# Attention and mixture-of-experts kernel: early shared loads, gated halves, an overflow branch moved ahead of the late stage, late sums in 2 KB pieces

## The chip, the cores and the metric

The kernel runs on one core of one Trainium2 chip, as one launch. The metric is device time in microseconds of that core. A measurement of this kernel can tell a change of about 0.3% from no change.

## What is computed

The input is x of shape (4, 1024, 256) in float32. Cut to what matters, the reference is:

```python
# power attention, 8 key heads, 2 query heads each, d = 128
a = where(causal, (q @ k.T * scale)**2 * exp(gate), 0)
y = (a @ v) / (sum(a) + 1e-6)
x = layernorm(x + y @ Wc + bc)
# mixture of experts over N = 4096 rows: 64 experts, top 6, capacity 768, F = 176
scores = softmax(x @ gate_w.T);  w, idx = top_k(scores, 6);  w = w / (sum(w) + 1e-20)
y = sum over the chosen experts of w * (silu(x @ wg.T) * (x @ wu.T)) @ wd.T
# shared expert over all rows, FS = 352
s = (silu(x @ sg.T) * (x @ su.T)) @ sd.T
out = layernorm(x + y + s)
```

## The kernel before, in words

Every product of float32 numbers is split into a rounded high part and the rest. `product` (L936) makes three TensorE passes for one product, and `down_passes` (L945) five for the down projection, where two rest parts share the array. All tiles sit in eight banks of PSUM: banks 0 to 5 hold gate and up results, three for each of two hidden units, and banks 6 and 7 are the spare pair, used in turn by everything else.

`schedule()` writes one list, `order`, of tasks, by hand. Each engine has a program (`sp_program`, `pe_program`, `act_program`, `dve_program`, `pool_program`) that walks the same list and runs those tasks that it has a part in. So the order of the list is the order on every engine, and what an engine waits for stands in its own instructions, as semaphore waits through `Once`. A task that waits holds up all that follows on its engine.

The stages in order are these.

- **Attention.** Units of scores and values, for four batches of eight heads. In the last two heads the routing of the batch before, and of the first half of the last batch, runs in the background, one step for each unit: statistics, normed rows, their transpose `x1t` (stored to DRAM as `x1t_dram`), logits, softmax, top 6, one-hot counts, slots, and for each half the steps `again` and `send`, whose rows POOL scatters into the experts' `slots` (L2284).
- **Shared stage.** Six blocks m of 512 rows. Each block has two hidden units k = 2m and 2m + 1, 12 in all. `up(k)` is three parts of six passes (TensorE). `hidden(k, part)` is the gate, in four parts: part 0 silu of the first 128 hidden rows (ACT), part 1 multiplication (DVE) and high part (ACT), part 2 silu of the last 48 rows (ACT), multiplication and rest of the first part (DVE), part 3 high and rest of the last 48 (`hb`, ACT then DVE). `shared_end(m)` is two `shared_down` of 20 matmuls each, eviction by ACT into `y_e`, and the store. `shared_in(m)` loads a block's transposed rows; XE = 4 buffers hold blocks 0 to 3, of which block 0 is loaded in the last attention units and blocks 1 to 3 after `attention_over` (L1138). Between these, `route_to(...)` runs the routing of the second half of the last batch, and two steps rank the experts by their counts.
- **Expert stage.** 68 places; at each, `up`, `hidden`, the transposes of the next expert's rows, and the `down` of the one before. ACT weighs and evicts the results, and POOL adds them to the output's rows by indirect DMA (L2294). At place 8 `rank_counts` finds whether any expert has more rows than its place holds, into `over_count`, and POOL loads that number into a register (L2303).
- **Late stage.** Two more blocks of the shared expert (ML = 2, units KL to KR - 1), in the order up, hidden, up, hidden, two `late_down`.
- **Overflow.** `overflow` (L2479 to L2497) on PE, ACT, DVE and POOL: wait for `o_done`, load the count (POOL has it already), branch. With a count over 0 the rest rows are worked; else `skip` sets the semaphores. For these inputs the count is 0, so the way taken is the far one, over the whole body.
- **Block sums.** SP loads each block's two partial results (L1188 to L1190), POOL adds them (L2365), DVE makes statistics (L2201 to L2226), ACT norms (L1758 to L1767), SP stores. There are six blocks of four rows per partition and four of two; the last four take rows in an order that makes the pieces 1 KB.

Of the kernel before, what the change touches and what calls it, by code (L numbers as in the profile page):

```python
# [182 lines left out]
def schedule():  # L183
# [81 lines left out]
    early_at = {12: ("raw_in", SHARED[0]), 13: ("raw_in", SHARED[1]), 14: ("shared_in", 0), 17: ("split_hi", SHARED[0]),  # L265
# [49 lines left out]
    for u, (n_, g, s) in enumerate(UNITS_ALL):  # L315
# [94 lines left out]
    assert not background  # L410

    second = route_steps(B)
    tail = [item[1:] for item in late]
    assert tail == [("project", HEADS - 1, NG - 2), ("turn", HEADS - 1, NG - 1), ("project", HEADS - 1, NG - 1)], tail
# [27 lines left out]

    catch_up()
    up(0, 0)
    do("experts_begin")
    send_all()
    hidden(0, 0)
# [4 lines left out]
    hidden(0, 1)  # L452
    on_spare("project", HEADS - 1, NG - 2)
    hidden(0, 2)
# [3 lines left out]
    hidden(0, 3)  # L458
    route_to("stat0")
    up(1, 1)  # L460
    do("add", HEADS - 1, NG - 1)
    for m in range(1, XE):
        do("shared_in", m)
    route_to("std")
    up(1, 2)
    hidden(1, 0)
    route_to("store")
    up(2, 0)
    route_to("x1t0")
    hidden(1, 1)  # L470
    up(2, 1)
    route_to("logit0")
    hidden(1, 2)
    route_to("x1t1")
    up(2, 2)
    hidden(1, 3)
    route_to("logit1")
    do("rank_keys")
    shared_end(0)
    on_spare("rank_experts")  # L480
    do("raw_in", MAINS[0])
    route_to("softmax0")
    up(3, 0)
    hidden(2, 0, 1)
    route_to("softmax1")
    up(3, 1)
    route_to("max")
    up(3, 2)
    hidden(2, 2, 3)
    route_to("index")  # L490
    up(4, 0)
    route_to("chosen0")
    up(4, 1)
    hidden(3, 0, 1)
    up(4, 2)
    route_to("chosen1")
    hidden(3, 2, 3)
    shared_end(1)
    do("raw_in", MAINS[1])
    route_to("weight1")  # L500
    hidden(4, 0, 1)
    up(5, 0)
    route_to("count")
    hidden(4, 2, 3)
    up(5, 1)
    route_to("slots")
    route_to("send0")
    up(5, 2)
    hidden(5)
    route_to("send1")  # L510
    assert not second
    for m in range(2, M1):
        if m + 1 < M1:
            for k in (2 * m + 2, 2 * m + 3):
                up(k)
                hidden(k)
        shared_end(m)
        if m in (2, 3):
            do("split_hi", MAINS[m - 2])
            for part in range(3):  # L520
                do("split_lo", MAINS[m - 2], part)
# [20 lines left out]
    for place, x_id in enumerate(SEQ):  # L542
# [4 lines left out]
        if place == 8:  # L547
            on_spare("rank_counts")
            do("load_count")
# [27 lines left out]
    if not ML:  # L577
        down(SEQ[-1], (0, 1))
    for d in range(ML):
        for k in (KL + 2 * d, KL + 2 * d + 1):  # L580
            up(k)
            hidden(k)
            if k == KL:
                down(SEQ[-1], (0, 1))
# [48 lines left out]
def build(nc, xT, x, wall, wvall, wg, gw, bc, wffn, table, out):  # L633
# [45 lines left out]
    N_SPARE = len(spare)  # L679

# [17 lines left out]
    with ExitStack() as ctx:  # L698
# [52 lines left out]
        over_count = sb(ctx, "over_count", [1, 1], I32)  # L751
# [220 lines left out]

        def rows_of(x_id):
# [53 lines left out]
        def sp_program(e):  # L1027
# [81 lines left out]
            def route(p, name):  # L1109
# [4 lines left out]
                elif name[:3] == "x1t":  # L1114
# [3 lines left out]
                    e.dma_start(x1t_dram[0, :, :, ts], f32(x1t_hi[:, :, :])).then_inc(s_x1t_out, 16)  # L1118
                    once.wait_ge(*out_of(("route", p, name)))
                    e.dma_start(x1t_dram[1, :, :, ts], f32(x1t_lo[:, :, :])).then_inc(s_x1t_out, 16)  # L1120
# [62 lines left out]
            def rows_of_block(whole, n):  # L1183
                at = sum(BLOCK_ROWS[:n]) * P
                order_ = "(p j) c -> p j c" if n < M1 else "(j p) c -> p j c"
                return whole[at:at + BLOCK_ROWS[n] * P, :].rearrange(order_, p=P)
# [26 lines left out]
        def pe_program(e):  # L1213
            once = Once(e)

# [1345 lines left out]
```

## Time and profile before

| what | value |
|---|---|
| time, median of 3 runs | 2263.62 us (2263.26 to 2268.72) |
| the profiled execution's own time | 2266.61 us |
| its span in the trace | 2264.8 us |
| TensorE busy in the span | 2151.7 us, 95% |
| mean granted clock of TensorE | 0.975 of full |
| VectorE, ScalarE, GpSimd busy | 1286.2, 1157.8, 751.3 us |
| shared stage, as it is cut below | 1619.0 to 1742.5 us |
| expert stage, from the first down to the last add | 1760 to 2214 us |

Busy time of an engine is the sum of its instructions; a line of the 40 slices of the page shows where in the span it is low. TensorE is at nine tenths or more in nearly every slice; it falls to seven or eight in the slices of the shared stage, and to two in the last one, where only the block sums are left. An engine name with a q behind it (POOLq, ACTq) is its sequencer: branches, register loads and semaphores.

### The profile page before, as it was taken

What the parts mean: (1) busy time and instruction counts of PE and PEld (TensorE: products, weight loads), DVE (VectorE), ACT (ScalarE), POOL (GpSimd) and SP (SyncE); (2) the same over time, 40 slices, a digit from 0 to 9 for tenths busy, and PEclk for the clock granted to TensorE, in tenths of its full rate; (3) what the DMA queues carried; (4) which work ended last, traced back from release to release, by engine and by line L of the source; (5) the groups of instructions that cost most, each with busy time, mean ns of one, the idle gap of its engine ahead of it and who ended that gap; (6) DMA issues with size and microseconds to landing.
All of it is one profiled execution on the core that took longest, in us unless ns stands there. A gap on an engine that the chain in (4) does not pass through costs nothing.

```text
span 2264.8 us, 38662 instructions
## 1 busy us (share of the span) xinstructions
PE 2151.7 (95%) x14567; PEld 1967.5 (87%) x14570; DVE 1286.2 (57%) x2851; ACT 1157.8 (51%) x2201; POOL 751.3 (33%) x751
## 2 busy tenths in 40 slices
PE   8999999999999999999999999999879899999992
PEld 6999998999989899888989898998767889999982
DVE  4444444454666445465644556545654688888865
ACT  4544545444444445444444444444324677877764
POOL 3121112100004510000452002430214578878883
PEclk9999999999999999999999999999889999999996
DMA  5876722122112411211241211322244789999966
GB/s 171 335 274 263 294 102 71 46 63 71 43 52 98 138 49 54 81 35 59 92 141 53 80 53 54 104 78 70 76 165 150 194 214 235 235 229 235 230 126 230
DMA packets 148180, 302.30 MB, mean 133 GB/s; under 512 B 20336, under 2 KB 85616, under 8 KB 147984
## 3 DMA queue, kind: packets, MB, share of 16 engines
q1 hardware_dynamic: 106496, 247.34, 32.3%
q0 software_dynamic: 41056, 51.96, 11.5%
q8 instruction: 117, 1.92, 0.3%
q14 instruction: 79, 0.65, 0.1%
q10 hardware_dynamic: 432, 0.44, 0.1%
HBM read 160.57 MB, written 142.67 MB: 134 GB/s over the span
## 4 chain that ended last, share of the span: by engine, by line
PE 84%; DVE 7%; ACT 4%; issue 3%; DMA 1%; POOL 1%; SPq 0%; ACTq 0%; DVEq 0%; POOLq 0%
PE bank L936 51%; PE bank L1331 21%; PE bank L945 7%; PE bank L1344 2%; PE bank L1448 2%; DVE ub L1876 1%; DVE bank L2061 1%; DVE bank L2058 1%; ACT silu_b L1664 0%; POOL slots L2284 0%; DVE stats L2210 0%; ACT wf_hi L1648 0%; ACT q_hi L1591 0%; ACT xe_hi L1675 0%; ACT x1t_hi L1633 0%
## 5 line engine op out<-in xcount | busy, mean ns | idle before, releaser
L1331 PEld LDWEIGHTS bank<-v,a 128*128 128x128 f32 x4608 | 605.2, 191 | 43.6 <-ACT a L1615 0.5
L1331 PE MATMUL bank<-v,a 128*128 128x129 f32 x4608 | 618.4, 275 | 0.3 <-ACT a L1615 0.3
L2294 POOL DMA_INDIRECT y_part<-y_e,row_token x234 | 360.2, 1539 | 123.9 <-issue 62.6
L2267 POOL TENSOR_TENSOR decay_all<-decay_all,tab 128x128 f32<-128x128 f32 x128 | 59.5, 465 | 918.6 <-DMA decay_all<-decay_dram 918.3
L1611 ACT ACTIVATE a<-bank,c_s 128x512 f32<-128x512 f32 x384 | 263.1, 686 | 183.6 <-PE bank L936 170.8
L1615 ACT ACTIVATE a<-ub 128x512 f32<-128x512 f32 (+1 forms) x256 | 133.8, 523 | 376.9 <-DVE ub L1876 370.6
L2284 POOL DMA_INDIRECT slots<-rows,slot_u x192 | 188.5, 982 | 336.9 <-DVE slot_u L2041 154.2
L936 PE MATMUL bank<-q_hi,k_hi 128*128 128x512 f32 (+1 forms) x640 | 262.6, 410 | 7.5 <-DVE ub L1876 7.5
L1855 DVE TENSOR_TENSOR q_lo<-bank,q_hi 128x512 fp32r<-128x512 f32 x128 | 88.5, 692 | 271.4 <-ACT q_hi L1591 271.3
L936 PE MATMUL bank<-q_lo,k_hi 128*128 128x512 f32 (+1 forms) x640 | 238.3, 372 | 0.0
L936 PE MATMUL bank<-q_hi,k_lo 128*128 128x512 f32 (+1 forms) x640 | 237.2, 371 | 0.0
L936 PE MATMUL bank<-xe_hi,wf_hi 128*128 128x512 f32 (+8 forms) x504 | 192.3, 382 | 18.5 <-DVE hb L2066 9.2
L936 PE MATMUL bank<-xe_lo,wf_hi 128*128 128x512 f32 (+8 forms) x504 | 185.6, 368 | 0.0
L936 PE MATMUL bank<-xe_hi,wf_lo 128*128 128x512 f32 (+8 forms) x504 | 185.4, 368 | 0.0
L936 PE MATMUL bank<-xt_hi,w_hi 128*128 128x512 f32 x384 | 166.4, 433 | 2.4 <-DVE acc L1916 1.3
L936 PE MATMUL bank<-wc_hi,yt_hi 128*128 128x256 f32 x512 | 155.1, 303 | 3.6 <-DVE yt_lo L1906 3.6
L1916 DVE TENSOR_TENSOR acc<-bank,acc 128x512 f32<-128x512 f32 x128 | 88.2, 689 | 116.9 <-PE bank L936 116.7
L936 PE MATMUL bank<-xt_hi,w_lo 128*128 128x512 f32 x384 | 151.2, 394 | 0.0
L936 PE MATMUL bank<-xt_lo,w_hi 128*128 128x512 f32 x384 | 150.8, 393 | 0.0
L1876 DVE TENSOR_TENSOR ub<-bank,em 128x512 f32<-128x512 f32 (+1 forms) x256 | 140.8, 550 | 16.4 <-PE bank L936 8.8
L936 PE MATMUL bank<-wc_hi,yt_lo 128*128 128x256 f32 x512 | 145.3, 284 | 0.0
L936 PE MATMUL bank<-wc_lo,yt_hi 128*128 128x256 f32 x512 | 145.1, 283 | 0.0
(231 smaller groups left out, 4766.3 us busy)
## 6 DMA issues: line engine op xcount, KB each, us to landing
slots<-acc SPq DMA_DIRECT2D x64, 816.0 KB, 7.8
w_raw_f<-in_wffn SPq DMA_DIRECT2D x68, 624.0 KB, 5.1
decay_all<-decay_dram SPq DMA_DIRECT2D x128, 128.0 KB, 3.1
xr<-slots SPq DMA_DIRECT2D x18, 544.0 KB, 5.5
xr<-slots SPq DMA_DIRECT2D x20, 476.0 KB, 5.3
w_hi<-w_dram SPq DMA_DIRECT2D x24, 384.0 KB, 4.4
w_lo<-w_dram SPq DMA_DIRECT2D x24, 384.0 KB, 5.1
wc_hi<-wc_dram SPq DMA_DIRECT2D x24, 256.0 KB, 2.6
```

What stands on the lines that cost most here:

```text
L936: ins = e.matmul(dst, a, b, start=first and i == 0, stop=last and i == len(passes) - 1, skip_group_check=True)
L945: ins = e.matmul(dst, a, b, start=first and n_ == 0 and p_ == 0, stop=n_ == len(steps) - 1 and p_ == len(passes) - 1, skip_group_check=True)
L1331: ins = e.matmul(dst[:, tt, r, :], a32[u % NA][:, r, t0:t0 + P], v[n % 3][:, s, :], start=(s == 0 and r == 0), stop=(s == 2 * g + tt), ski ...
L1344: ins = e.transpose(ps[:, r, tt * P:(tt + 1) * P], yn[j % YR][:, tt, r, :], ident)
L1611: e.activation(squares, score_bank(u)[:, 0:R * w].rearrange("p (r t) -> p r t", r=R), ACT.Square, scale=c_s[b % 2][:, g * (g - 1) + s, h:h ...
L1615: e.activation(squares, ub[masked_nth[u] % 2][:, :, 0:w], ACT.Square).then_inc(s_sq)
L1855: e.tensor_tensor(lo, bank[6 + m % 2][:, :], f32(hi), ALU.subtract).then_inc(s_out_of[m % 2])
L1876: e.tensor_tensor(ub[mine % 2][:, :, 0:w], score_bank(u)[:, 0:R * w].rearrange("p (r t) -> p r t", r=R), decay.unsqueeze(1).to_broadcast([ ...
L1916: e.tensor_tensor(part, bank[6 + m % 2][:, :].rearrange("p (t c) -> p t c", c=C), part, ALU.add).then_inc(s_out_of[m % 2])
L2267: e.tensor_tensor(arg[:, GROUP:GROUP + P], arg[:, P:GROUP], mask, ALU.add)
L2284: e.indirect_dma_start(out=slots, out_offset=bass.IndirectOffsetOnAxis(ap=slot_u[:, j, k:k + 1], axis=0), in_=rows[:, j, :], in_offset=Non ...
L2294: e.indirect_dma_start(out=y_part[part], out_offset=bass.IndirectOffsetOnAxis(ap=token, axis=0), in_=y_rows, in_offset=None, bounds_check= ...
```

## The change

The first shared rows are loaded earlier. `shared_in(1)` goes to attention unit 37 and waits only for the last scores, `shared_in(2)` goes right ahead of the first `up`, and `shared_in(3)` behind the last `add`. The last part of the first half's routing (`again1`, `send1`) is held back from the attention units and done behind `shared_end(0)`. In the shared stage `gated` takes the place of `hidden`: both silus in part 0, both multiplications in part 1 on DVE, high parts on ACT and rests on DVE behind. The two transposes `x1t0` and `x1t1` of the second half stand side by side, the second in the buffers `yt_hi[0]` and `yt_lo[0]`, and the order of `up`, `gated`, `shared_end` and the routing steps is written anew; both ranking steps stand behind the last `send`. From block 2 on the eviction of a shared down also waits for all stores of `x1t`.

`over_count` becomes `no_rest`, 1 where the count is 0. All four engines load it at place 8 of the expert stage. PE, ACT and DVE branch ahead of the late stage, and POOL behind its last add: the way with `no_rest` stands directly behind the branch, holds the late stage and the block sums, and ends in a jump over the other way, which holds the same again with the overflow between. The late stage's order becomes up, hidden, last expert down, up, hidden, up, two `late_down`, hidden, up, hidden, two `late_down`. The late hidden units are written by tile, so that a partition holds neighbouring rows and the late pieces of sums and output are 2 KB.

```diff
--- before.py
+++ after.py
-    early_at = {12: ("raw_in", SHARED[0]), 13: ("raw_in", SHARED[1]), 14: ("shared_in", 0), 17: ("split_hi", SHARED[0]),
+    early_at = {12: ("raw_in", SHARED[0]), 13: ("raw_in", SHARED[1]), 14: ("shared_in", 0), 37: ("shared_in", 1), 17: ("split_hi", SHARED[0]),
...
-        elif background and u >= step_from:
+        elif background and u >= step_from and background[0] != (B - 1, "again1"):
...
+    def gated(k, *parts):
+        for part in parts or range(4):
+            do("gated", k, part)
+
     catch_up()
+    do("shared_in", 2)
     up(0, 0)
     do("experts_begin")
     send_all()
     up(0, 1)
     on_spare("turn", HEADS - 1, NG - 1)
     do("turn_lo", HEADS - 1, NG - 1)
     up(0, 2)
+    gated(0, 0)
     on_spare("project", HEADS - 1, NG - 2)
+    gated(0, 1)
     up(1, 0)
     do("add", HEADS - 1, NG - 2)
     on_spare("project", HEADS - 1, NG - 1)
     route_to("stat0")
+    gated(0, 2, 3)
     up(1, 1)
     do("add", HEADS - 1, NG - 1)
+    do("shared_in", 3)
     route_to("std")
     up(1, 2)
+    gated(1, 0)
     route_to("store")
+    gated(1, 1)
     up(2, 0)
     route_to("x1t0")
+    on_spare("route", *second[1])
+    x1t1 = second.pop(1)
+    gated(1, 2, 3)
     up(2, 1)
     route_to("logit0")
     up(2, 2)
     route_to("logit1")
+    route_to("softmax0")
+    shared_end(0)
+    for step in background:
+        route_step(*step)
+        send_all()
+    gated(2, 0)
+    route_to("max")
+    gated(2, 1, 2, 3)
+    up(3)
+    route_to("index")
+    route_to("chosen0")
+    gated(3, 0)
+    up(4)
+    gated(3, 1, 2, 3)
+    route_to("chosen1")
+    shared_end(1)
+    route_to("weight1")
+    gated(4, 0)
+    up(5, 0)
+    gated(4, 1, 2, 3)
+    route_to("count")
+    up(5, 1, 2)
+    route_to("slots")
+    route_to("send0")
+    up(6)
+    gated(5)
+    shared_end(2)
+    route_to("send1")
+    assert not second
     do("rank_keys")
     on_spare("rank_experts")
     do("raw_in", MAINS[0])
     do("raw_in", MAINS[1])
+    up(7)
+    gated(6)
+    for m in range(3, M1):
+        up(2 * m + 2) if m + 1 < M1 else None
+        gated(2 * m + 1)
+        shared_end(m)
         if m + 1 < M1:
+            up(2 * m + 3)
+            gated(2 * m + 2)
+        if m in (3, 4):
+            do("split_hi", MAINS[m - 3])
             for part in range(3):
+                do("split_lo", MAINS[m - 3], part)
...
+    do("late",)
+    for k in range(KL, KR):
+        up(k)
+        if k == KL:
             hidden(k)
-            if k == KL:
-                down(SEQ[-1], (0, 1))
-        if d + 1 < ML:
-            do("late_in", d + 1)
-        for pair in range(MAIN // GROUP):
-            on_spare("late_down", d, pair)
+            down(SEQ[-1], (0, 1))
+            continue
+        if (k - KL) % 2 == 0:
+            for pair in range(MAIN // GROUP):
+                on_spare("late_down", (k - KL) // 2 - 1, pair)
+        hidden(k)
+        if (k - KL) % 2 and (k - KL) // 2 + 1 < ML:
+            do("late_in", (k - KL) // 2 + 1)
+    for pair in range(MAIN // GROUP):
+        on_spare("late_down", ML - 1, pair)
     return order, spare
...
+        def rows_first(k):
+            return MT if k >= KL and k < KR else 1
+
+        def in_order(by):
+            return (lambda a: a.rearrange("p (t j) -> p t j", j=by)) if by > 1 else (lambda a: a)
+
+        def by_tile(by):
+            return (lambda a: a.rearrange("p (j t) -> p t j", j=by)) if by > 1 else (lambda a: a)
...
-                if m:
+                if m >= XE:
                     attention_over(once)
+                elif m:
+                    once.wait_ge(s_scores, len(UNITS_ALL))
+                    if m > 1:
+                        values_over(once)
...
+                m, half = (n, None) if n < M1 else (M1 + (n - M1) // 2, (n - M1) % 2)
+                in_rows = whole[m * MAIN:(m + 1) * MAIN, :].rearrange("(p j) c -> p j c", p=P)
+                return in_rows if half is None else in_rows[:, 2 * half:2 * half + 2, :]
...
+            def load_count():
+                nonlocal fits
+                once.wait_ge(c_count, 1)
+                fits = e.value_load(no_rest[0:1, 0:1], min_val=0, max_val=1)
...
+            passed = dict(once.passed)
+            with e.If(fits > 0):
+                late()
+            with e.Else():
+                once.passed = passed
+                late()
+                overflow(e, once, over_body, over_skip, over_settled)
...
+            def gated(k, part):
+                b0, i = 3 * (k % 2), k % HS
+                if part == 0:
+                    if k == 0:
+                        values_over(once)
+                    once.wait_ge(c_gu, 3 * k + 1)
+                    if k:
+                        once.wait_ge(c_h, 2 * k)
+                    e.activation(silu_a[:, :], bank[b0][:, :], ACT.Silu).then_inc(c_silu)
+                    once.wait_ge(c_gu, 3 * k + 3)
+                    e.activation(silu_b[:, :], bank[b0 + 2][0:FB, :], ACT.Silu).then_inc(c_silu)
+                elif part == 1:
+                    once.wait_ge(c_h, 2 * k + 1)
+                    hidden_free(once, k)
+                    e.activation(ha_hi[i][:, :], bank[b0 + 1][:, :], ACT.Copy).then_inc(c_hh)
+                elif part == 2:
+                    once.wait_ge(c_h, 2 * k + 2)
+                    once.wait_ge(c_zero, HS)
+                    e.activation(hb[i][0:FB, :], bank[b0 + 2][0:FB, :], ACT.Copy).then_inc(c_hh)
...
+                if m_ >= 2:
+                    once.wait_ge(s_x1t_out, 16 * 2 * NG * B)
...
-                e.tensor_copy(over_count[:, :], rank_col[0:1, 0:1]).then_inc(c_count)
+                e.tensor_scalar(no_rest[:, :], rank_col[0:1, 0:1], 0.0, None, ALU.is_equal).then_inc(c_count)
...
+            with e.If(fits > 0):
+                e.sem_inc(o_done, E)
+                sums()
...
+        def x1t_of(p, k):
+            return (yt_hi[0], yt_lo[0]) if (p, k) == (B, 1) else (x1t_hi, x1t_lo)
...
```

## Rows read from the trace of the kernel before

**Rows 1.** The page, part 4: shares by engine of the chain that ended last

```profile
PE 84%; DVE 7%; ACT 4%; issue 3%; DMA 1%; POOL 1%; SPq 0%; ACTq 0%; DVEq 0%; POOLq 0%
```

**Rows 2.** Windows: us, length, busy PE PEld DVE ACT POOL, PEclk, DMA share, GB/s

```profile
1619.00:1742.50 123.50, 100.00 (x530) 84.94 (x527) 68.19 (x141) 44.00 (x72) 49.38 (x53) 0.88 0.42 146
```

**Rows 3.** Waits of PE, shared stage: waiting line, releaser, us, times, longest

```profile
PE bank L936 <- DVE hb L2066: 9.2, 3, 4.6
PE bank L936 <- DMA xe_lo<-x1t_dram: 7.7, 1, 7.7
PE bank L936 <- DVE x1t_lo L1955: 3.5, 1, 3.5
```

**Rows 4.** Chain of work, shared stage: start, us, what, matmuls

```profile
1640.37 2.93 PE bank L936 x6
...
1680.51 6.57 PE bank L945 x40
...
1706.71 4.80 PE bank L945 x40
...
1724.61 8.30 PE bank L936 x36
```

**Rows 5.** Timeline, one hidden unit, first silu to last rest

```profile
1717.88 0.58 ACT L1657 ACTIVATE silu_a<-bank 128x512 f32<-128x512 f32 x1
...
1721.99 0.68 DVE L2066 TENSOR_TENSOR hb<-bank,hb 48x512 fp32r<-48x512 f32 x1
```

**Rows 6.** Timeline, first units of the shared stage

```profile
1629.04 1.95 POOL L2291 MEMSET hb<- 112x512 f32 x4
...
1635.67 1.38 DVE L1948 TENSOR_SCALAR rows<-acc,mv,rstd 128x256 f32<-128x256 f32 x4
```

**Rows 7.** Chain, two of DVE's routing steps

```profile
1672.78 0.97 DVE onehot L1991
...
1676.76 1.53 DVE chosen L1999
```

**Rows 8.** Chain, first expert weights behind the shared stage

```profile
1749.25 3.88 DMA w_raw_f<-in_wffn
```

**Rows 9.** Timeline of POOL, last of the second half's 24 scatters

```profile
1727.06 1.29 POOL L2284 DMA_INDIRECT slots<-rows,slot_u  x1 [0.30 <-issue]
```

**Rows 10.** Timeline, line L2303 and chain: the count's way at place 8

```profile
1800.46 0.27 PE L1481 MATMUL bank<-rank_hot,count_col 128*1 128x64 f32 x2
...
1801.39 0.14 DVE L2111 CAST over_count<-rank_col 1x1 int32<-1x1 f32 x1
...
L2303 POOLq TENSOR_LOAD <-over_count x1: 673/673/673, 1803.4 to 1803.4; - x1
...
1806.91 4.16 DMA y_part<-y_e,row_token
```

**Rows 11.** Lines of POOL's sequencer: its branch and what follows

```profile
L2486 POOLq COMPARE_BRANCH  x1: 53/53/53, 2214.7 to 2214.7; - x1
...
L2357 POOLq EVENT_SEMAPHORE  x1: 17/17/17, 2217.3 to 2217.3; - x1
```

**Rows 12.** Timeline of the block sums, and ACT's sequencer at the end

```profile
2222.21 2.38 POOL L2365 TENSOR_TENSOR w_raw_f<-w_raw_f,wf_hi 128x1024 f32<-128x1024 f32 x1 [7.58 <-DMA wf_hi<-y_part]
...
2232.72 1.40 DVE L2210 BATCH_NORM_STATS2 stats<-w_raw_f 128x6 f32<-128x256 f32 x4 [15.79 <-DVEq L2189]
...
2234.57 2.15 DVE L2217 TENSOR_SCALAR std<-mv 128x4 f32<-128x4 f32 x1
...
2241.96 2.48 POOL L2365 TENSOR_TENSOR xr<-xr,acc 128x512 f32<-128x512 f32 x2
...
2246.23 0.17 DVE L2217 TENSOR_SCALAR std<-mv 128x4 f32<-128x4 f32 x1
...
2260.35 0.16 DVE L2226 SCALAR_TENSOR_TENSOR row_rec<-mv,rstd 128x2 f32<-128x2 f32 x1
...
L698 ACTq DRAIN  x1: 1744/1744/1744, 2260.6 to 2260.6; - x1
```

More of the change, by code:

```diff
@@ L409, in schedule @@
                 do("x_rest", b1, x_split_at.index(at))
-    assert not background
     second = route_steps(B)
-    tail = [item[1:] for item in late]
-    assert tail == [("project", HEADS - 1, NG - 2), ("turn", HEADS - 1, NG - 1), ("project", HEADS - 1, NG - 1)], tail
+    left = [item[1:] for item in late]
+    assert left == [("project", HEADS - 1, NG - 2), ("turn", HEADS - 1, NG - 1), ("project", HEADS - 1, NG - 1)], left
+    assert [name for _, name in background] == ["again1", "send1"], background
     def send_all():
@@ L446, in schedule @@
     send_all()
-    hidden(0, 0)
     up(0, 1)
@@ L495, in schedule @@
[L495 to L498, printed above, removed]
-    do("raw_in", MAINS[1])
[L500 to L512, printed above, removed]
-        if m + 1 < M1:
[L514 to L519, printed above, removed]
+    do("raw_in", MAINS[1])
@@ L679, in build @@
     N_SPARE = len(spare)
+    LATE_AT = order.index(("late",))
     read_until = {}
@@ L1487, in pe_program, with late @@
             once.wait_ge(s_const, 48)
-            for what, *which in order:
+            for what, *which in order[:LATE_AT]:
                 if what in parts:
                     parts[what](*which)
+            def late():
+                for what, *which in order[LATE_AT:]:
+                    if what in parts:
+                        parts[what](*which)
             def over_body(q):
@@ L1718, in act_program, with late @@
             e.dma_start(gw_raw[:, :, :], gw).then_inc(s_const, 16)
-            for what, *which in order:
+            for what, *which in order[:LATE_AT]:
                 if what in parts:
                     parts[what](*which)
+            def late():
+                for what, *which in order[LATE_AT:]:
+                    if what in parts:
+                        parts[what](*which)
             def over_body(q):
@@ L1768, in block_norm, with blocks @@
                 ins.then_inc(d_norm)
-            for n in range(BLOCKS + 1):
-                if n < BLOCKS:
-                    block_root(n)
-                if n:
-                    block_norm(n - 1)
+            def blocks():
+                for n in range(BLOCKS + 1):
+                    if n < BLOCKS:
+                        block_root(n)
+                    if n:
+                        block_norm(n - 1)
+            passed = dict(once.passed)
+            with e.If(fits > 0):
+                late()
+                blocks()
+            with e.Else():
+                once.passed = passed
+                late()
+                overflow(e, once, over_body, over_skip, over_settled)
+                blocks()
         def dve_program(e):
@@ L2155, in dve_program, with late @@
             e.tensor_tensor(gw_lo[:, :, :], gw_raw[:, :, :], f32(gw_hi[:, :, :]), ALU.subtract).then_inc(s_tab)
-            for what, *which in order:
+            for what, *which in order[:LATE_AT]:
                 if what in parts:
                     parts[what](*which)
+            def late():
+                for what, *which in order[LATE_AT:]:
+                    if what in parts:
+                        parts[what](*which)
             def over_body(q):
@@ L2226, in block_rstd, with blocks @@
                 e.scalar_tensor_tensor(out=shift, in0=mv_[:, :, 0], scalar=-1.0, in1=rs, op0=ALU.mult, op1=ALU.mult).then_inc(d_rstd)
-            for n in range(BLOCKS + 1):
-                if n < BLOCKS:
-                    block_stats(n)
-                if n:
-                    block_rstd(n - 1)
+            def blocks():
+                for n in range(BLOCKS + 1):
+                    if n < BLOCKS:
+                        block_stats(n)
+                    if n:
+                        block_rstd(n - 1)
+            passed, steps_so_far = dict(once.passed), done
+            with e.If(fits > 0):
+                late()
+                blocks()
+            with e.Else():
+                once.passed, done = passed, steps_so_far
+                late()
+                overflow(e, once, over_body, over_skip, over_settled)
+                blocks()
         def pool_program(e):
             once = Once(e)
-            count = None
+            fits = None
             def acc_add(b, half):
```

157 lines of the change are left out of this document (78 added, 79 removed).

## The prediction

> **What bounds the kernel now.** I read the shares of the chain on the page first. TensorE carries 84% of it, VectorE 7%, ScalarE 4% [rows 1]. So a step of this change is worth what it takes from a time in which TensorE idles or runs at its low clock, or from the end, where TensorE has nothing left. The slices show two such places, the shared stage and the last slice. I read each from its own views.
>
> The window of the shared stage is 123.5 us long with 100.0 us of TensorE work in it, so 23.5 us are idle, at a mean granted clock of 0.88 [rows 2]. The waits name the idle time: 7.7 us for the second block's rows by DMA, three waits of 9.2 us together for DVE's last rest `hb`, 3.5 us for `x1t_lo` [rows 3]. The chain gives the price of the work at the full clock: 36 passes take 8.30 us, so one `up` takes 4.15, and 40 matmuls of a `shared_down` take 4.80 [rows 4]. Twelve ups are 49.8, six downs 28.8, and the turn, two projections, transposes, logits and counts between them some 7.7 (an estimate, from their columns at the same pace): 86.3 us. The 13.7 us up to 100.0 are what the low clock costs. It is seen directly: behind the 7.7 us gap six passes took 2.93 us where 1.38 is the full pace, and a down behind another gap took 6.57 instead of 4.80, so it lost 1.8 [rows 4].
>
> At the end, SP may load the sums only when POOL has passed its branch; the branch stands at 2214.7 and the next instruction at 2217.3, 2.6 us later [rows 11]. POOL's first sum starts at 2222.21, DVE's first statistics at 2232.72, after a wait of 15.79 us [rows 12]. DVE had its last late unit done at about 2216.9 and stood behind its own branch, 10.5 us after the first sum began.
>
> **Shared stage, S.** I walked the new list engine by engine with the old durations.
>
> - Start. The rows of block 1 are asked for 15 to 20 us earlier, so the wait of 7.7 us goes. What is late next is the routing: POOL's clearing of `hb` runs to 1631.0, DVE's rest behind it to 1632.4, and only then statistics and rows, which end at 1637.05 [rows 6]. The first half's scatters ahead of the clearing stay the same, so neither moves. TensorE has its first two ups done at 1632.5 as now, then one part of `up(2)` (1.38 us) to 1633.9, and then stands at the first transpose until 1637.05: 3.2 us. Waits of 1.3 us for the last attention group's norm before that stay.
> - Behind it DVE, in list order, does the gate and the routing. One gate took 4.8 us from the first silu to the last rest [rows 5]; with both silus ahead the chain is silu, two multiplications, rest, rest, 3.4 us (0.6 and four times 0.7). `softmax0` and the held back `again1`, `send1` (3.1 us of DVE work: a one-hot of 0.97 and three reductions of about it) lie beside `shared_end(0)`. Before `shared_end(1)` DVE has two one-hots of 0.97 and two sums of 1.53 [rows 7] and two gates of 2.8 each: 10.6 us, with softmax and top 6 ahead of it, against `shared_end(0)` and two ups on TensorE. I get TensorE ready at 1658.8 and `hb` at 1662.2: 3.4 us idle. Before `shared_end(2)` 0.9, before `shared_end(4)` 0.6.
> - The last `shared_end(5)` has no up behind the last one to cover its gate: 3.4 plus the split of weights on ACT ahead of it, 1.25: 4.6 us idle.
>
> Idle together: 1.3 + 3.2 + 3.4 + 0.9 + 0.6 + 4.6 = 14.0. The two gaps of before with a row behind them were followed by the low clock, so I give it to the three gaps above 3 us; each costs between 1.8 (the slow down) and about 3 (twice the 1.55 of the six passes) [rows 4], I take 2.7: 8.1. The stage then lasts 86.3 + 14.0 + 8.1 = 108.4, and S = 123.5 - 108.4 = 15.1. It arrives at the experts in full if their first weights keep their distance: they are asked for behind the last store of the stage, at 1749.25 [rows 8], and the diff leaves that order as it is. The 24 scatters, at 1.28 us each until 1728.3 [rows 9], start with their slots some 20 us earlier and stay ahead of the stage's end. I keep S between 8 (half the DVE steps slip) and 20 (only the 3.2 and 4.6 stay).
>
> **The count on four engines, L.** At place 8 POOL alone loaded the count. Now PE, ACT and DVE wait too, and all that follows on them is queued behind. From the matmul (1800.46, ends 1800.7) to the end of the cast is 0.8 us; the load took 673 ns on POOL, with some 0.2 of register steps: TensorE is stopped for about 1.8 us [rows 10]. At the upper end the low clock follows and costs as much again, 3.6, and twice the load would be 6. At the lower end some is absorbed: at 1806.91 the chain itself runs for 4.16 us through one of POOL's adds [rows 10], so TensorE waits there a little anyhow; below nothing is excluded, since the wait only adds. I take 2.5, range 0 to 6. In return the late loads of the count at the overflow go, off the path except in the next part.
>
> **Late stage and block sums, T.** POOL falls through its branch, so SP starts 2.4 us earlier and the first sum is there at about 2219.8 to 2222.2. DVE and ACT no longer jump at 2226 and DVE can start with the first sum's end, 2222.2 instead of 2232.7. These 10.5 us don't all arrive: while POOL adds, DVE is held. A `std` of four elements took 2.15 us while a POOL sum ran, and 0.17 once POOL was done [rows 12]; so a four-row block took 3.7 to 4.1 us of DVE beside POOL and 2.2 to 2.6 alone. POOL adds until 2244.4 [rows 12], in the new kernel until about 2241. From 2222.2 DVE does some five blocks beside it, and then the rest alone: about 12.2 us for one block of four and four of two, with the last steps: it ends near 2254.4 instead of 2260.5. T = 6.1, between 0 and 10. The Trainium skill ("SBUF — State Buffer", section "Who interferes with whom") says the same of this pair: the engine that comes second is fully blocked by an exclusive lock. The row of 2.15 us agrees, and this is what speaks against reading 10.5 us from the wait.
>
> The jump moves to the end: the way taken closes with one over the other way. ACT's last sequencer step starts at 2260.6 while the kernel's end comes at 2264.8 [rows 12], because the last store is awaited; a jump of 2.6 [rows 11] is covered by that, so nothing to 2.3 us. The Trainium skill ("Runtime: NRT & Kernel Launch", section "Instruction fetch mechanics") states that a taken branch to a target outside the loaded pages stalls for a fetch. The 2.6 us of POOL agree; by this rule the change doesn't remove a jump but moves it. Late hidden units written by tile stride their outputs; even at one and a half times their 0.7 us this hides in the late stage, where DVE is not bound, and 2 KB pieces make SP's issues cheaper. I count both at nothing.
>
> **Sum.** -15.1 + 2.5 - 6.1 = -18.7. From the profiled execution's 2266.61 us that gives 2247.9. It lies 3.0 above the median of the runs, 2263.62, so 2244.9, and I predict 2245.
>
> **Rivals.**
>
> - B, DVE's routing stays the bound. The wait for the DMA turns into the 3.2 us for the rows, the 3.5 us for `x1t_lo` goes, the waits of 9.2 for `hb` stay with their low clock. For it: DVE is busy 68 us in the stage and it works in list order. S = 7.7 - 3.2 + 3.5 = 8.0, time 2252. Chance 0.16.
> - D, the tail gives nothing: POOL's and DVE's block work together is the bound, or the closing jump is exposed. T = 0, time 2251. Chance 0.12. With B together 2258, chance 0.07.
> - F, more: the early sums end sooner by the 2 KB pieces (POOL waits less between its sums) and the shared stage loses only 3.2 and 4.6: time 2233 to 2239. Chance 0.10.
> - C, slower: with shorter but more numerous gaps TensorE stays at its low clock over a share f of the stage's 86.3 us of work, each us of it costing one more. Now 13.7 of 86.3 are lost, f = 0.16; forecast 0.09. With 14.0 idle and L and T as above the change gives nothing at f = 0.31 and is slower by over 0.3% from f = 0.39; at f = 0.5 the time is 2283 - 3 = 2280. For it: the mean of 0.88 [rows 2]; against it: ups of full clock follow each other for 30 us at the stage's end [rows 4]. Chance 0.05.
>
> **How the numbers follow.** The forecast, 2239 to 2250, has 0.50. About 0.3% is what a measurement of this kernel can tell from no change, 6.8 us: below 2256.8 is faster, above 2270.4 slower. Faster: 0.50 + 0.16 + 0.12 + 0.10 less 0.02 for the upper tails of B and D, 0.86; within 0.09; slower 0.05. For 8 in 10 the range leaves out half of F, most of B with D, and C: 2238 to 2257.
>
> **What would show it.** Right: no wait for `xe_lo`; a wait of about 3 us at the first transpose; stage length near 108; TensorE idle 1.8 us at place 8; DVE's first statistics at POOL's first sum, with `std` near 2 us beside POOL. Wrong: `hb` waits above 10 us together (B), a last statistics step 42 us or more behind POOL's branch (D; now 45.8), a clock under 0.85 in the stage (C), or waits of several engines at place 8 that last beyond 6 us.

## The result and the profile after

The changed kernel takes 2247.02 us (median of 5 runs, 2238.76 to 2249.72) against 2263.62 us; the ratio is 0.9912, 95% interval 0.9888 to 0.9936. A second measurement of the same code beside the experiments, called the control below, gave 2244.34 us (2241.09 to 2248.00), ratio again 0.9912. The forecast was 2245 us, faster than before, between 2238 and 2257.

The profiled execution took 2248.40 us, its span is 2246.6. Three marks cut each span into the terms of the sum: the last score-value pass, the eviction of the last shared down, and POOL's `over_flag` memset behind its last add. The marks are rounded to 0.1 us.

| stretch | before | after | difference | forecast |
|---|---|---|---|---|
| start to the last score-value pass | 1617.3 | 1621.3 | +4.0 | 0 |
| to the eviction of the last shared down (S) | 125.2 | 109.9 | -15.3 | -15.1 |
| to POOL's memset behind its last add (L) | 472.0 | 474.4 | +2.4 | +2.5 |
| to the end (T) | 50.3 | 41.0 | -9.3 | -6.1 |
| span | 2264.8 | 2246.6 | -18.2 | -18.7 |

The shared stage by windows (start:end, length, busy PE, PEld, DVE, ACT, POOL, granted clock, DMA share, GB/s), first before and then after, both from mark to mark ([rows 2] starts 1.7 us later), and a stretch of the attention stage, again before and then after:

```profile
1617.30:1742.50 125.20, 101.04 (x534) 85.79 (x534) 69.82 (x145) 44.00 (x72) 49.38 (x53) 0.88 0.42 144
...
1621.30:1731.20 109.90, 93.09 (x536) 79.62 (x537) 71.27 (x145) 44.24 (x72) 50.32 (x53) 0.95 0.48 163
...
768.00:900.00 132.00, 129.44 (x903) 117.61 (x902) 64.50 (x153) 63.44 (x114) 29.66 (x38) 1.00 0.21 69
...
768.00:900.00 132.00, 129.44 (x888) 117.33 (x887) 64.08 (x153) 63.01 (x114) 29.19 (x37) 0.99 0.19 66
```

The changed kernel's stage has 16.8 us idle at a clock of 0.95, where before had 24.2 us idle and 101.0 us busy at 0.88. So 7.4 us of S are idle time, and 7.9 us are the same work at a higher clock. In the stretch of attention nothing was changed, yet the clock is 0.99 in the second line; the stretch 1170 to 1300 shows the same. These drops, and a start 0.7 us later (POOL's `xt_lo` at 367.4 against 366.7), account for the +4.0 of the first row of the table. They come and go between executions: the profiles of load_late, one_kb and raw_early, whose attention list is the same, have 1.00 in both stretches. The control has both drops and still reaches the mark at 1615.7: its `xt_lo` stands at 365.2, and its clock from 1580 to 1600 is 1.00, where it is 0.74 in before and in the changed kernel.

Waits of PE in the stage, answering to [rows 3]:

```profile
PE bank L953 <- DVE hb L2167: 10.3, 4, 4.7
PE bank L944 <- DVE hb L2167: 3.0, 2, 1.5
PE bank L1397 <- DVE rows L2031: 2.7, 1, 2.7
PE bank L1366 <- DVE yn L1981: 0.7, 1, 0.7
```

The 7.7 us for `xe_lo` and the 3.5 us for `x1t_lo` are gone. Of the waits for the routing 2.7 us for `rows` are new. The waits for `hb` are 13.3 us in all. That is 2.2 more than before, where a down waited for it too, besides the 9.2 us of [rows 3]:

```profile
PE bank L945 <- DVE hb L2066: 1.9, 1, 1.9
```

Where the waits of the changed kernel stand shows in the timeline of PE (start, duration, operation, in brackets the idle time ahead and what ended it):

```profile
1636.39 0.47 PE L944 MATMUL bank<-xe_hi,wf_hi 128*128 128x512 f32 x1 [1.50 <-DVE hb L2167]
...
1640.73 1.94 PE L1397 MATMUL bank<-tab,rows 128*128 128x128 f32 x8 [2.72 <-DVE rows L2031]
...
1659.05 0.47 PE L944 MATMUL bank<-xe_hi,wf_hi 128*128 128x512 f32 x1 [1.51 <-DVE hb L2167]
...
1665.44 0.39 PE L953 MATMUL bank<-wf_hi,ha_hi 128*128 128x256 f32 x1 [2.03 <-DVE hb L2167]
...
1682.57 0.39 PE L953 MATMUL bank<-wf_hi,ha_hi 128*128 128x256 f32 x1 [3.29 <-DVE hb L2167]
...
1723.98 0.58 PE L953 MATMUL bank<-wf_hi,ha_hi 128*128 128x256 f32 x1 [4.73 <-DVE hb L2167]
...
1748.88 0.55 PE L953 MATMUL bank<-wf_hi,ha_hi 128*128 128x256 f32 x1 [7.84 <-DVE xe_lo L2236]
...
1788.94 0.42 PE L944 MATMUL bank<-xe_hi,wf_hi 128*128 128x336 f32 x1 [1.74 <-DVE no_rest L2212]
```

The line at 1723.98 is the last shared down without an up over its gate. That at 1748.88 is the first expert's down, and that at 1788.94 is TensorE behind the load of the count. The block sums, answering to [rows 11, 12]:

```profile
L2491 POOLq COMPARE_BRANCH  x2: 40/40/41, 2205.5 to 2231.1; - x2
...
2210.74 2.40 POOL L2487 TENSOR_TENSOR w_raw_f<-w_raw_f,wf_hi 128x1024 f32<-128x1024 f32 x1 [5.10 <-DMA wf_hi<-y_part]
...
2217.96 2.34 POOL L2487 TENSOR_TENSOR w_raw_f<-w_raw_f,wf_lo 128x1024 f32<-128x1024 f32 x1 [1.39 <-DMA wf_lo<-y_part]
...
2230.59 2.48 POOL L2487 TENSOR_TENSOR xr<-xr,acc 128x512 f32<-128x512 f32 x2
...
2213.17 1.41 DVE L2319 BATCH_NORM_STATS2 stats<-w_raw_f 128x6 f32<-128x256 f32 x4 [6.80 <-POOL w_raw_f L2487]
...
2215.03 1.57 DVE L2326 TENSOR_SCALAR std<-mv 128x4 f32<-128x4 f32 x1
...
2218.46 1.87 DVE L2326 TENSOR_SCALAR std<-mv 128x4 f32<-128x4 f32 x1
...
2220.44 0.16 DVE L2335 SCALAR_TENSOR_TENSOR row_rec<-mv,rstd 128x4 f32<-128x4 f32 x1
...
2222.37 0.52 DVE L2326 TENSOR_SCALAR std<-mv 128x4 f32<-128x4 f32 x1
...
2241.91 0.16 DVE L2335 SCALAR_TENSOR_TENSOR row_rec<-mv,rstd 128x2 f32<-128x2 f32 x1
```

POOL passes its branch in place: SP's first load starts at 2205.67, 0.2 us behind it, where before it was 2.6 us. POOL's first sum starts 5.2 us behind the memset, not 7.7. DVE starts right behind that sum's end. From there to DVE's last step it is 28.9 us.

### The profile page after: what moved, and what is told of

Same layout as the page of the kernel before. It is cut to its first block, busy times and chain, and to the rows that moved or that the text cites. A ratio compares the mean times of both kernels' runs of the same rounds, so it can differ in the third digit from the quotient of the medians.

```text
span 2246.6 us, 38647 instructions
## 1 busy us (share of the span) xinstructions
PE 2141.0 (95%) x14570; PEld 1957.3 (87%) x14570; DVE 1292.5 (58%) x2851; ACT 1162.2 (52%) x2201; POOL 752.3 (33%) x751
## 3 DMA queue, kind: packets, MB, share of 16 engines
q0 software_dynamic: 41056, 51.96, 11.7%
## 4 chain that ended last, share of the span: by engine, by line
PE 83%; DVE 7%; ACT 3%; issue 3%; POOL 2%; DMA 2%; SPq 0%; ACTq 0%; POOLq 0%; DVEq 0%
PE bank L944 50%; PE bank L1353 21%; PE bank L953 7%; PE bank L1366 2%; PE bank L1471 2%; DMA y_part<-y_e,row_token 1%; DVE ub L1959 1%; POOL y_part L2414 1%; DVE stats L2319 0%; ACT wf_hi L1688 0%; POOL slots L2404 0%; ACT q_hi L1631 0%; DVE bank L2146 0%; DVE wf_lo L2131 0%; DVE bank L2143 0%
```

## Experiments

Each is an edit of the changed kernel. They ran in three groups on three chips, each with the kernel before beside it (2265.3, 2264.3 and 2265.7 us), so times of different groups compare within some 2 us. By their times alone only tail_alone, old_gate and late_rows (slower), raw_early (narrowly) and all_five (faster) lie outside the control's 2241.09 to 2248.00; what is said of the others is read from their profiles. Stage lengths are cut at the marks of the table, from one profile each. In kernels that don't touch them the shared stage lay between 109.9 and 112.0 us, the end between 40.2 and 41.0, and the expert stage between 472.6 and 478.1. So a difference of 2 us in the expert stage is not read from its length alone.

**Undo the shared stage (tail_alone).** The shared stage's list, gates and loads of before, with the new end:

```diff
-    do("shared_in", 2)
     up(0, 0)
...
-    gated(0, 0)
+    hidden(0, 1)
...
+    for m in range(1, XE):
+        do("shared_in", m)
```

> The change without its part in the shared stage: rows of blocks 1 to 3 asked for, gates, routing and order as before; the count on four engines, the branch ahead of the late stage and the 2 KB pieces stay. My theory: the three parts of the sum are independent, so the stage lasts 125 us again (from the last score-value pass to the last down, 109.9 in the changed kernel) and the time is 2247 + 15 = 2262, with expert stage and end as in the changed kernel. Rival: the new tail gains because the stage's scatters and loads come earlier; then the end falls back too and the time is near 2269 or above.

Measured: 2257.51 us (2254.12 to 2263.47), ratio to before 0.9973. The stage took 124.2 us and the end 40.2. The waits are those of [rows 3] again, 7.7, 9.2 and 3.5 us. So the new end works without the new stage and the rival falls; the two gains are separate. The time is 4 us under my figure and 13 above the control, where S is 15. In its profile the attention stage ended at 1613.2, 8 us earlier than in the changed kernel's, so the profiled times compare only stretch by stretch.

**Undo the gate's order (old_gate).**

```diff
     def gated(k, *parts):
         for part in parts or range(4):
-            do("gated", k, part)
+            do("hidden", k, part)
```

> The changed kernel with the gate's old inner order in the shared stage (one silu, multiplication, high part, second silu, multiplication, rests), at the same places of the list. My theory: one gate's chain is 3.4 us with both silus ahead and 4.8 us without, so the three waits for its last rest that stand before a down (2.0, 3.3 and 4.7 us) grow by about 1.4 each: 2247 + 4 = 2251, in the trace waits for hb of 16 to 18 us instead of 13.3. Rival: VectorE's list is the bound there and the chain's inner order costs nothing: 2246 to 2248, waits unchanged.

Measured: 2253.11 us (2248.71 to 2261.49); the stage took 120.2 us, 10 more. The waits of PE:

```profile
PE bank L953 <- DVE hb L2151: 14.5, 4, 6.9
PE bank L944 <- DVE hb L2151: 6.9, 5, 2.6
```

That is 21.4 us against 13.3 in the changed kernel. The rival falls: the order inside the gate counts. My size was half of it, because I looked only at the downs. The second line shows that ups wait too, five times now, since they write the banks that the gate still reads.

**Load the rows late (late_rows).**

```diff
-    do("shared_in", 2)
     up(0, 0)
...
-    do("shared_in", 3)
+    for m in range(1, XE):
+        do("shared_in", m)
     route_to("std")
```

and unit 37's `shared_in(1)` out, each again behind `attention_over`.

> The changed kernel with the loads of the rows of blocks 1 to 3 back behind the last add, all else as changed. My theory: the wait for xe_lo comes back at the first up of block 1, some 7 us, in place of the 1.5 and part of the 2.7 that stand there now, with its low clock: 2247 + 5 = 2252 (3 to 9 more). Rival: the routing of the second half is what is late there anyhow (rows, transposes), so the load is hidden by it and the time stays within 1 us.

Measured: 2252.98 us (2249.30 to 2254.68); stage 118.0, 8.1 more.

```profile
PE bank L944 <- DMA xe_lo<-x1t_dram: 8.8, 1, 8.8
PE bank L944 <- DVE hb L2163: 1.5, 1, 1.5
```

The wait is back, 8.8 us, and in its place the 2.7 us for `rows` and one of the two 1.5 us for `hb` are gone. The early loads are worth 6 to 8 us of the stage, given the 109.9 to 112.0 of kernels that keep them.

**Don't hold the routing back (no_hold).**

```diff
-        elif background and u >= step_from and background[0] != (B - 1, "again1"):
+        elif background and u >= step_from:
```

> The changed kernel with the last part of the first half's routing back in the attention units. My theory: 3.1 us of VectorE work and 12 scatters go from behind the first shared down to the last attention units, where the last norm waits for it by 0.6 to 1.2 us, and they no longer stand ahead of the waits of 1.5 and 2.0 us at the second down: the two nearly cancel, -2 to +1, time 2245 to 2248. Rival: held back it was worth its 3 us, since the last norm and with it the clearing of hb move: 2250.

Measured: 2245.90 us (2243.91 to 2246.67), stage 110.0. As the first theory had it, this part of the change gives nothing that shows: the last norm waits 1.2 us in place of 0.7 and `yt_lo` 0.7, and one of the waits of 1.5 us for `hb` goes.

**Load the count behind (load_late).** `load_first` is POOL's load, `load_count` that of PE, ACT and DVE:

```diff
         if place == 8:
             on_spare("rank_counts")
-            do("load_count",)
+            do("load_first",)
...
+    do("load_count",)
     do("late",)
```

> The changed kernel with the load of the count on PE, ACT and DVE moved from place 8 to right ahead of the branch before the late stage; POOL keeps its load at place 8. My theory: the term L is a real stop of TensorE, 1.74 us of waiting for no_rest plus the low clock of 3.4 us behind it; at the branch the number is long there and POOL's adds are the bound, so the load hides. The expert stage, last shared eviction to POOL's last memset, goes from 474.4 back to 472 or a little below, time 2247 - 2.5 = 2244.5. Rival: the stop was absorbed by the waits for POOL's adds that follow it, and its place doesn't matter: 474, time 2247.

Measured: 2241.58 us (2239.37 to 2244.61); expert stage 473.2, end 41.0. Windows of 15 us from the count's matmul on, first the changed kernel, then this one:

```profile
1786.90:1801.90 15.00, 13.26 (x78) 12.13 (x78) 9.78 (x26) 9.34 (x18) 8.80 (x6) 0.89 0.85 193
...
1781.80:1796.80 15.00, 14.04 (x95) 12.52 (x95) 12.13 (x32) 10.57 (x22) 10.30 (x8) 1.00 0.86 194
```

TensorE is busy for 14.04 us instead of 13.26, at full clock instead of 0.89. The stop and the low clock behind it are real and go. What they cost in time isn't settled: the expert stage of 473.2 lies between 474.4 and the control's 472.6, and the time, 2241.6 against 2244.3, is inside the spread of the runs. It is between nothing and some 3 us.

**1 KB pieces (one_kb).** `rows_first` gives 1 and `rows_of_block` is that of before.

> The changed kernel with the late hidden units and the late sums in the old order of rows, pieces of 1 KB. My theory: of the 9.3 us that the end became shorter (50.3 to 41.0 from POOL's memset to the end), the early start of SP, POOL and DVE carries nearly all; the pieces only make SP's last loads slower, and the last two sums of POOL come 1 to 2 us later: end 42 to 43, time 2247 + 1.5. Rival: the 3.1 us by which I under-sized the end are the pieces': end 44 or more, time 2250.

Measured: 2245.50 us (2244.63 to 2246.32); end 40.4. Neither theory's loss is there. SP's last six loads take 9.6 us to issue instead of 8.5, and POOL's first sum starts 5.9 us behind its memset instead of 5.2, but DVE's way from that sum to its last step is shorter by as much or more, so the end is no later. One profile can't say whether the two belong together.

**Epsilon on ACT (std_on_act).**

```diff
-                e.activation(sd, sd, ACT.Sqrt).then_inc(s_sqrt)
+                e.activation(sd, mv_[:, :, 1], ACT.Sqrt, bias=eps_col[:, 0:1]).then_inc(s_sqrt)
...
-                step(ins)
-                steps_done()
-                e.tensor_scalar(sd, mv_[:, :, 1], LN_EPS, None, ALU.add).then_inc(s_std)
+                ins.then_inc(s_std)
```

> The changed kernel with DVE's addition of epsilon in the block sums (tensor_scalar of 4 or 2 elements, 0.5 to 1.9 us while POOL adds, 0.17 alone) taken off DVE; ACT's root adds it as its bias. My theory: these steps wait for POOL's adds on the shared way into the memory, and without them DVE keeps POOL's pace: its last step comes 2 to 3.5 us earlier, end 41.0 - 2.5, time 2244.5. Rival: the wait is not in the operation but in being beside POOL, so the next operation of DVE (reciprocal, or the product for the shift, which takes 1.1 already) takes it over: end 40.5 to 41, time 2246.5.

Measured: 2243.04 us (2237.20 to 2244.55); end 38.2, which is 2.0 to 2.8 us shorter than in kernels that don't touch it. The timeline of DVE:

```profile
2217.16 0.15 DVE L2333 RECIPROCAL rstd<-std 128x4 f32<-128x4 f32 x1
2217.34 1.88 DVE L2335 SCALAR_TENSOR_TENSOR row_rec<-mv,rstd 128x4 f32<-128x4 f32 x1
2219.24 1.41 DVE L2321 BATCH_NORM_STATS2 stats<-w_raw_f 128x6 f32<-128x256 f32 x4
```

Both were half right. The hold did move to the next such operation, `row_rec`, which had taken 0.16; but one hold in place of up to two gives those 2.0 to 2.8 us. It is the operation that is held: statistics and reciprocal beside it keep their length.

**First expert's weights early (raw_early).**

```diff
         gated(2 * m + 1)
+        if m == M1 - 1:
+            do("raw_in", MAINS[2])
         shared_end(m)
...
-    do("raw_in", MAINS[2])
     turn(SEQ[0])
```

> The changed kernel with the load of the first expert's weights asked for ahead of the last shared down, not behind the stage's last store and loads. It tests the claim that the stage's end hands its gain to the experts through a fixed distance set by SP's list. My theory: the weights then lie ready, ACT splits them 5 us earlier, and TensorE's wait of 7.8 us at the first expert down shrinks to about 3: expert stage 474.4 - 5 = 469.5, time 2242. Rival: rows, transposes and the first gate are late there anyhow: 472 to 473, time 2245.

Measured: 2238.33 us (2235.30 to 2240.64); expert stage 469.8.

```profile
1735.72 0.55 PE L954 MATMUL bank<-wf_hi,ha_hi 128*128 128x256 f32 x1 [2.41 <-DVE xe_lo L2237]
```

The wait of 7.84 us is 2.41, and the first expert's down starts 12.2 us behind the stage's mark, where it was 17.7. SP's list did set the distance between the stages.

**Second expert's split behind the last gate (split_behind).** `split_hi` and `split_lo` of `MAINS[1]` move from behind block 4 to ahead of the last `shared_end`.

> The changed kernel with the split of the second expert's weights (1.15 us of ACT, 1.6 us of DVE) put behind the last gate instead of ahead of it. My theory: it is what makes the last uncovered gate 4.7 us long; without it TensorE waits 2.0 to 2.3 us less before the last shared down, so the wait is 2.4 to 2.7, stage 110.0 - 2.3 = 107.7, time 2244.5. Rival: the split is only moved onto the first expert's path, where its gate waits for it: stage shorter, expert stage longer by the same, time 2247.

Measured: 2243.55 us (2235.07 to 2246.22), stage 107.4, and the last wait for `hb` 2.85 instead of 4.73 us. The expert stage took 479.1, the longest of all, and the time is the control's within the spread. The first expert doesn't take the gain back: its down starts 18.0 us behind the stage's mark, against 17.7. Whether the later ones do stays open.

**Clear `hb` first (clear_first).** First-half scatters wait in the list until `experts_begin`:

```diff
-        if to_send and (at in send_at or n >= LAST):
+        if to_send and to_send[0][1] != B - 1 and (at in send_at or n >= LAST):
```

> The changed kernel with all 12 scatters of the first half's first part put behind POOL's clearing of hb, which before stood behind six of them. It tests the step that POOL's clearing is what is late next once the rows are there early. My theory: the clearing then ends some 7 us earlier, VectorE's first hb rest and the routing's rows move 4 us forward, the waits of 1.5 and 2.7 us go and with them a drop of the clock: stage 110.0 - 5, time 2242.5. Rival: the last projection and its addition (done at about 1634) hold the rows by themselves, and little moves: 1 us or less.

Measured: 2243.37 us (2240.20 to 2246.45), stage 107.7. The first wait of 1.5 us for `hb` is gone, and the one for `rows` is 1.5 instead of 2.7:

```profile
PE bank L1397 <- DVE rows L2031: 1.5, 1, 1.5
```

So the clearing did hold the rows, as the prediction said, but only part of the wait; the rest is VectorE's own list from addition to rows.

**The control (after_again).** The changed kernel, unedited.

> The changed kernel, unedited, as a control on the same chip as the next three. Expected 2247 within 3 us; a profiled run whose attention stage has no short drop of the clock should end that stage 3 to 4 us earlier than the first profile (last score-value pass at about 1617 instead of 1621), with the other stages unchanged (110, 474, 41). If the attention stage were 4 us longer by the change itself, it would be 1621 in every profile.

Measured: 2244.34 us; last score-value pass at 1615.7, then 110.6, 472.6 and 40.3 us. The two short drops that I had expected to be missing are there, and the mark is early for two other reasons, an earlier start and the clock from 1580 to 1600. In the profiles of all kernels with this attention list it lies between 1613.6 and 1621.3, with 1617.3 in before: nothing shows the attention stage longer by the change.

**Five edits together (all_five).**

> The changed kernel with five edits together: count loaded late on three engines, first expert's weights asked for early, second expert's split behind the last gate, epsilon added by ACT, clearing of hb ahead of the scatters. If the terms add: stage 110.0 - 2.3 - 4 = 103.7, expert stage 474.4 - 4.6 - 1.2 = 468.6, end 41.0 - 2.8 = 38.2, together 15 us less than the changed kernel: 2232, between 2227 and 2237. Rival: the stage's last gate and the first expert share ACT and DVE, so two of the edits give one gain: 2236 to 2240.

Measured: 2232.27 us (2225.10 to 2234.51), ratio to before 0.9841, interval 0.9816 to 0.9865, against 0.9912 (0.9886 to 0.9938) for the changed kernel in the same runs. Stage 105.9, expert stage 470.9, end 38.2. It beats both kernels, by 12 us the changed one. Against the changed kernel's first profile the shared stage gained 4.0 us of the 6.3 that I added up, the expert stage 3.5 of 5.8, and the end its 2.8. Clearing and split leave the waits of 1.5, 2.0 and 3.3 us for `hb` where they were. What each edit gives within the five isn't shown.

## Why the prediction held, and where its steps were off

The time came out 2 us above the forecast (the control 1 us below it). Of the four stretches S and L came out in the size forecast. That the sums agree so well is partly luck: T gave 3.2 us more than I had, and 4.0 us of attention, which no step of mine held, took that back. The steps were these.

**S, 15.3 against 15.1.** The size is right, its parts are not. I had the idle time fall by 9.5 us (23.5 to 14.0) and the low clock give back 5.6. It was 7.4 and 7.9. Three steps are behind this.

First, the wait at the first transpose came as forecast, 2.7 against 3.2, but there is one of 1.5 ahead of it. I kept 1.3 us of waits for the last attention group, 0.57 for its norm and 0.69 for `yt_lo`, and neither came; no_hold has both back, so it is the held back routing that took them out. So the first two ups were done 13.6 us behind the mark instead of 15.4 and met POOL's clearing, which had not moved (11.6 us behind it, 11.7 before).

Second, the waits of 3.4, 0.9 and 0.6 ahead of downs are in truth 1.5 ahead of an up and 2.0, 3.3 and 0.3 ahead of downs, the largest one block later than I had it.

Third, I priced each gap above 3 us at 2.7 us of low clock. Two shared downs of the changed kernel, from the chain of work, and one of before, from PE's timeline:

```profile
1682.57 5.06 PE bank L953 x40
...
1723.98 7.21 PE bank L953 x40
...
1680.51 0.58 PE L945 MATMUL bank<-wf_hi,ha_hi 128*128 128x256 f32 x1 [1.86 <-DVE hb L2066]
```

The first stood behind the wait of 3.3 us and ran at a granted clock of 1.00. The second, the last down, lost 2.4 us at 0.66. Behind the 2.7 us for the rows, the first of my three gaps, the clock was 0.53 for 3 us. A mean of 0.95 over 109.9 us is a loss of some 5 us (an estimate), where I had 8.1. And the third line is the down of 6.57 us from which I took the lower price: the wait right ahead of it was only 1.9 us, and one of 4.6 us lay 9 us earlier. The length of the gap right ahead was the wrong measure; what the right one is stays open.

The last gap, 4.7 against 4.6, was right to a tenth. That the early rows carry a part of the gain is shown by late_rows (8.1 us of stage), and the gate's order by old_gate (10.2). Undone singly they sum to more than 15.3, so the two are not independent. The gain reaches the experts in full, as the prediction had it: the first expert's down starts 17.7 us behind the stage's mark in both kernels, at 1748.88 above and here before:

```profile
1760.21 0.55 PE L945 MATMUL bank<-wf_hi,ha_hi 128*128 128x256 f32 x1 [4.11 <-DVE xe_lo L2135]
```

**L, 2.4 against 2.5.** The stop was 1.74 us (forecast 1.8), with a low clock behind it. The experiment confirms the stop; the 2.4 us itself is within what this stage varies by, so the agreement is no proof.

**T, 9.3 against 6.1.** This is the term that was mis-sized. SP's earlier start, 2.5 us, and the closing jump, 0.2 us (from DVE's last step to the end it is 4.5 us, before 4.3), came as forecast, and DVE started with the first sum's end. No run puts the branch back, so its part is read from the rows alone. The Trainium skill ("Runtime: NRT & Kernel Launch", section "Instruction fetch mechanics") states that a taken branch to a target outside the loaded pages stalls for a fetch. Both rows agree: 0.2 us from POOL's branch to SP's first load where the way now falls through, 2.6 before, and at the end a jump that other waits cover.

The step that failed is "some five blocks beside POOL at 3.7 to 4.1 us". From the first sum's end to DVE's last step I had 32.2 us; it was 28.9. The first five blocks took 16.2 us, 3.2 each, where I had 20.0, and the rest 12.7 for 12.2. The rows of before came from a DVE that started when POOL had four sums done. In two of its three blocks beside POOL both small operations were held; these are the two of its second block (`row_rec` there is of the block ahead):

```profile
2238.48 1.11 DVE L2217 TENSOR_SCALAR std<-mv 128x4 f32<-128x4 f32 x1
...
2239.70 1.10 DVE L2226 SCALAR_TENSOR_TENSOR row_rec<-mv,rstd 128x4 f32<-128x4 f32 x1
```

A hold ends with POOL's sum, and so DVE falls into step with the sums: in the changed kernel each of the first five `std` ends within 0.04 us of the end of the sum beside it (2220.33 and 2220.30, the lines at 2218.46 and 2217.96 above). From the third block on little of a sum is left when `std` comes, and the first three `row_rec` start between two sums. `std` took 1.57, 1.87, and then 0.5 to 0.7, `row_rec` 0.16 three times and 1.1 twice. std_on_act agrees: the hold belongs to these operations, and with one kind less the end is 2.0 to 2.8 us shorter; all_five, with the same edit, ends at 38.2 again. The 2 KB pieces, to which I gave nothing here and a part of rival F, give nothing that one_kb shows.

The Trainium skill ("SBUF — State Buffer", section "Who interferes with whom") calls the lock exclusive, held for the whole instruction. The 1.88 us of `row_rec` in std_on_act, 0.16 when alone, agree: it ends at 2219.22, and POOL's sum beside it at 2219.21.

**The rivals.** B kept the waits for `hb` and had the stage 8 us shorter. The waits are there, 13.3 us, more than the 10 that I had named as its sign, and the stage is still 15 us shorter, since the other waits went and the clock rose: that sign was ill chosen. D fell with T at 9.3, C with a clock of 0.95. Late units written by tile made DVE's rests 1.22 us instead of 0.70, more than my one and a half times. It hid as said: one_kb, in the old order of rows, is not faster. The new order of the late stage has no run of its own.

**The first row of the table** has no step in the prediction: 4.0 us of attention, a stretch that differs by up to 5.6 us between two profiles of the same code.

## What to carry to other kernels

When a wait is taken out, list what was waiting behind it and when that gets done: here 8 us of DMA wait turned into 4 us for the routing, and the distance from the stage's end to the first expert's weights was set by the place of one load in SP's list, worth 5 us of that distance. Compare stages between fixed marks rather than whole spans, and take a control on the same chip, where the runs of one kernel spread over several microseconds. A rate read from an engine that is behind is not its rate when it keeps pace.

## What the runs showed of the hardware

Short drops of the granted clock come in an unchanged attention stage, where TensorE is busy for 129 of 132 us, in some executions and not in others. From 768 to 900 the clock was 1.00 in before, load_late, one_kb and raw_early, and 0.99 in the changed kernel and its control; from 1580 to 1600 it was 0.74 in before and in the changed kernel and 1.00 in the control. With these and a start 2.2 us apart the last score-value pass of the same code lay at 1621.3 in one profile and at 1615.7 in the other.

The wait right ahead of a shared down doesn't tell its clock: behind 3.3 us one ran at 1.00 and took 5.06 us, behind 1.9 us one of before took 6.57, and the full pace is 4.80.

While GpSimd adds 128x1024 numbers (2.34 us), an addition on VectorE of 128x4 numbers took up to 2.15 us and ended with the sum, against 0.17 alone; statistics of 1.40 us beside the same sums kept their length.
